# Keys and queries turned for a recurrence: one half of the partitions copied by ScalarE, the other by a transfer, and the order of steps laid out anew

## What is computed

```python
def step(S, inp):                      # S: [b, 16 heads, 2, 16]
    ct, st, kt, vt, bt = inp           # kt: the key of this token, 16 values a head
    S0, S1 = (S[:, :, 0], S[:, :, 1])
    Sd = jnp.stack([ct * S0 + st * S1, -st * S0 + ct * S1], axis=2)
    pred = jnp.einsum('bhsd,bhd->bhs', Sd, kt)
    Sn = Sd + bt * (vt - pred)[..., None] * kt[:, :, None, :]
    return (Sn, Sn)
_, Ys = jax.lax.scan(step, S0, xs)     # over all tokens, in order
retrieved = jnp.einsum('blhsd,blhd->blhs', Y, Q) * sel_C_gate[..., None]
```

## Time and profile before

| | us |
|---|---|
| median of 3 runs | 3696.65 (3696.49 to 3699.05) |
| the profiled execution | 3695.73 |
| its span, first to last instruction | 3693.9 |
| stage of layers 0 to 2 side by side | about 95 to 2143 |
| one unit in its steady part | 235.5 |

### The profile page before, as it was taken

The page is one execution under the profiler, slowest core; times in us unless marked ns, Lnnn a source line. Parts: engine busy times, 40 slices in busy tenths (PEclk is TensorE's granted clock), DMA queues, the critical chain, the costliest instruction groups (busy, mean ns, idle before and its releaser), DMA issues.

```text
span 3693.9 us, 39884 instructions
## 1 busy us (share of the span) xinstructions
PE 2537.0 (69%) x13729; PEld 1367.2 (37%) x13729; DVE 2599.1 (70%) x5721; ACT 1670.5 (45%) x3056; POOL 509.9 (14%) x530
## 2 busy tenths in 40 slices
PE   3587967768677687686633047773577787778788
PEld 1343333333333333333211012221355555555553
DVE  3478758989889889797877656664366666666663
ACT  1233343442534424345243224444366666666662
POOL 0000003030030200301111200003112121212120
PEclk9589778878678687796866567787699999999999
DMA  2000000100001000010000021102677777777651
GB/s 82 2 9 27 22 27 6 45 2 26 23 3 49 1 22 28 1 43 7 30 7 15 1 79 29 29 6 98 180 205 208 203 214 201 218 211 201 198 160 53
DMA packets 310336, 274.34 MB, mean 74 GB/s; under 512 B 16012, under 2 KB 285982, under 8 KB 309718
## 3 DMA queue, kind: packets, MB, share of 16 engines
q1 hardware_dynamic: 310134, 271.79, 25.4%
HBM read 149.39 MB, written 122.36 MB: 74 GB/s over the span
## 4 chain that ended last, share of the span: by engine, by line
DVE 36%; PE 30%; issue 14%; ACT 13%; POOL 5%; DMA 1%; SPq 1%; DVEq 0%; POOLq 0%; ACTq 0%
ACT t L1364 3%; DVE t L2496 3%; PE banks L2519 3%; PE banks L2563 3%; ACT t L2431 2%; PE banks L420 2%; DVE t L1147 1%; PE banks L2480 1%; POOL t L2463 1%; DVE t L787 1%; DVE t L1660 1%; DVE t L1664 1%; DVE t L2249 1%; ACT L145 1%; DVE t L786 1%
## 5 line engine op out<-in xcount | busy, mean ns | idle before, releaser
L2496 DVE CUSTOM_DVE_ANT_0 t<-banks,t 128x896 f32<-128x896 f32 (+7 forms) x512 | 381.8, 753 | 147.2 <-PE banks L2482 76.4
L2519 PE MATMUL banks<-ident,t 128*128 128x128 f32 x2304 | 392.4, 291 | 134.8 <-ACT xT L2534 46.2
L2507 ACT ACTIVATE t<-t 128x896 f32<-128x896 f32 (+7 forms) x512 | 398.6, 779 | 175.6 <-DVE t L2496 175.0
L2519 PEld LDWEIGHTS banks<-ident,t 128*128 128x128 f32 x2304 | 260.4, 145 | 242.1 <-ACT xT L2534 62.3
L2463 POOL TENSOR_TENSOR t<-t 128x512 f32<-128x512 f32 x96 | 122.3, 1274 | 797.0 <-DMA t<-relative_scratch 724.6
L1700 ACT ACTIVATE t<-t 128x16 f32<-128x16 f32 x256 | 82.6, 323 | 316.0 <-DVE t L1664 254.2
L2480 PE MATMUL banks<-t 128*128 128x512 bf16 (+3 forms) x768 | 216.1, 337 | 7.2 <-DVE t L2496 7.0
L145 ACT ACT_TABLE_LOAD x112 | 143.7, 1283 | 152.4 <-DVE t L578 32.2
L538 POOL TENSOR_TENSOR t<-t 128x512 f32<-128x512 f32 x28 | 50.2, 1793 | 993.3 <-ACT t L510 993.3
L1095 ACT ACTIVATE t<-banks 128x512 f32<-128x512 f32 x128 | 76.2, 595 | 219.6 <-PE banks L1061 219.3
L1066 PE MATMUL banks<-t 128*128 128x512 f32 x256 | 146.9, 657 | 37.4 <-DVE t L1143 31.4
(11 more groups left out here) (451 smaller groups left out, 6196.5 us busy)
## 6 DMA issues: line engine op xcount, KB each, us to landing
relative_scratch<-t SPq DMA_DIRECT2D x128, 512.0 KB, 5.1
t<-relative_scratch SPq DMA_DIRECT2D x128, 512.0 KB, 4.4
relative_scratch<-t SPq DMA_DIRECT2D x128, 256.0 KB, 5.4
t<-in_wmoe SPq DMA_DIRECT2D x64, 384.0 KB, 3.0
t<-relative_scratch SPq DMA_DIRECT2D x80, 256.0 KB, 2.9
t<-cut_scratch SPq DMA_DIRECT2D x192, 64.0 KB
cut_scratch<-t SPq DMA_DIRECT2D x8, 768.0 KB, 3.4
z_scratch<-t SPq DMA_DIRECT2D x8, 512.0 KB, 3.0
```

Source lines behind the costliest of these rows:

```text
L2496: nc.vector.tensor_tensor_reduce(s.s[z][:, 0:n], ps[:, b0:b0 + 1 + i // 4, :].rearrange("p b n -> p (b n)")[:, 0:n], s.bias[r][:, j, WIDE ...
L2507: nc.scalar.activation(s.s[z][:, 0:n], s.s[z][:, 0:n], ACT.Exp, scale=-1.0, bias=s.least[:, z:z + 1]).then_inc(*a.mark("weights", u))
L2519: nc.tensor.transpose(ps[:, 4 + c % 2, (t - lo) * P:(t - lo + 1) * P], s.s[u % NS][:, t * P:(t + 1) * P], k.ident[:]).then_inc(*e.mark("tu ...
```

## The change

ACT's copies are halved: each bank is copied once, to partitions 0 to 63, and with its loops turned round: for each token four neighbouring features, so that it writes 16 bytes at a stretch and reads PSUM at steps of 512 bytes. Partitions 64 to 127 of kc and qc are filled by one transfer each, issued by SP in a new part turn2_sp: keys after the last of the keys' copies, queries after the last of the queries'. DVE's first reads of keys and of queries wait for these transfers in place of the copies. The strings of PE, ACT, DVE and SP are new throughout; SP's has two more steps t in each unit, behind the stores of in2 and ahead of back's. The string of POOL is unchanged. Of the strings only SP's and the steady lines of ACT's stand here.

```diff
--- before.py
+++ after.py
@@ -1360,9 +1360,17 @@
             act.wait_ge(e, u, w, n)
             if u:
                 act.wait_ge(k.line("rec_dve"), "ret", u - 1)
-            for half in (slice(0, H2), slice(H2, P)):
-                nc.scalar.copy(out[half, :, d0:d0 + 4].rearrange("p t d -> p d t"),
-                               ps[0:H2, G0 + n].rearrange("p (d t) -> p d t", d=4)).then_inc(*a.mark(u, w, n))
+            nc.scalar.copy(out[0:H2, :, d0:d0 + 4], ps[0:H2, G0 + n].rearrange("p (d t) -> p t d", d=4)).then_inc(
+                *a.mark(u, w, n))
+
+
+def turn2_sp(k, s):
+
+    for u in range(UNITS0):
+        for w, x in enumerate((s.kc, s.qc)):
+            yield
+            k.sp.wait_ge(k.line("turn2_act"), u, w, 3)
+            k.nc.sync.dma_start(x[H2:], x[0:H2]).then_inc(*k.queue(f"both{w}").mark(u))
 
 
 
@@ -1586,7 +1594,7 @@
 
 
 def rec_dve(k, s, u):
-    nc, dve, v, a, n = k.nc, k.dve, k.line("rec_dve"), k.line("turn2_act"), u % 2
+    nc, dve, v, n = k.nc, k.dve, k.line("rec_dve"), u % 2
     stt, tt, copy, reduce = (nc.vector.scalar_tensor_tensor, nc.vector.tensor_tensor, nc.vector.tensor_copy,
                              nc.vector.tensor_reduce)
     if u == 0:
@@ -1610,7 +1618,7 @@
         tt(later[:, :, c], later[:, :, c + 1], dl[:, :, c], ALU.mult).then_inc(*v.mark())
     yield
     dve.wait_ge(v)
-    dve.wait_ge(a, u, 0, 3)
+    dve.wait_ge(k.queue("both0"), u)
     tt(rows[:, :, :, 0:DH2], kb, rep(s.coef[:, :, 0], 3, DH2), ALU.mult).then_inc(*v.mark())
     yield
     tt(s.kd[:], kb, rep(later[:, :, 1:], 3, DH2), ALU.mult).then_inc(*v.mark())
@@ -1676,7 +1684,7 @@
         tt(y[:, :, j], y[:, :, j], s.at, ALU.add).then_inc(*v.mark())
         prior = y[:, :, j]
     yield
-    dve.wait_ge(a, u, 1, 3)
+    dve.wait_ge(k.queue("both1"), u)
     tt(y[:, :, BS - 1], s.first[:, 1:, 0:DH2], qb[:, :, BS - 1], ALU.mult).then_inc(*v.mark())
     yield
     dve.wait_ge(v)
@@ -1768,57 +1776,57 @@
 TURNS_ACT = (
-    "emrraeraremaeraeerererermerereerererearerremreeriirrrriairiramiiriirriarriiiiriiiimmrimimgmgmgmttttttttmbmmggfgb"
-    "ggkmkfmmfafmfmmfmfeememerarearemareaeerererermerererereereraerreremreiirrrrriairiramiiriirriarriiiiriiiimmrimimg"
...
+    "bkfkafmfmmfmmfmmffeememearearemareaererererermerererereereraererremreirirrririariamriiirirriaririiiriiiimmrgmmig"
+    "igmmmttttmttttbgmgmgbggfkkmmmfafmmfmfmfmmfeeeemaeararermaeerreerremreerererererereareerremreirirrriririarariimri"
+    "mirrimmrariiriiiiiigmimiggttttttttmggbmgggmmbkfkafmfmmfmmfmmffeememearearemareaererererermerererereereraererremr"
...
 )
...
@@ -1829,7 +1837,8 @@
 )
 
 TURNS_SP = (
-    "ibwqqwwwqqwwwwwwwqwwwwwwwwwiiiqwwwwwwwwiiibqwwwwwwwwiiibqqwwwwwwwwiiibwwwwwwwwiiibwwwwwwwwiiibwwwwwiiibiiibb"
+    "btiwqqwwwqqwwwwwwwwqwwwwwwwwiiiqttwwwwwwwwiiittbqwwwwwwwwiiittbqqwwwwwwwwiiittbwwwwwwwwiiittbwwwwwwwwiiittbwwwww"
+    "iiibttiiitbtb"
 )
 
 
@@ -1923,7 +1932,7 @@
 
 
 def side_by_side_sp(k, s, keep):
-    in_turn(TURNS_SP, {"in2": inputs2_sp(k, s, keep), "experts": experts1_sp(k, s), "turn0": turn0_sp(k, s),
+    in_turn(TURNS_SP, {"in2": inputs2_sp(k, s, keep), "experts": experts1_sp(k, s), "turn0": turn0_sp(k, s), "turn2": turn2_sp(k, s),
                        "back": back_sp(k, s, keep)})
```

More of the change, by code:

```diff
@@ L1776 @@
[L1776 to L1780, removed]
@@ L1781 @@
-    "eaaaaeaeaeeaaieeeeaeeeeeeeeeeeeeeeeeeeeeeeeeeeeeeeeeeeeeeeeeeeeeeeeiiiiiiittttbtttbtggaaaaiiiiiiiittttbtttbtggbb"
+    "bfatgmiemmmfmmmmmmffffmmfffmmmmfmmmmmmfmmfmmmmmmmmmmmmmmmmemfmmffffmfffmfmmfmfmmeemmammmmmmemmaammmmmmmmaemaeeem"
+    "eeeeeeeeeeemmemmmemmemeememeeeeeeeemmmmmemmemeeeeemeeeemmeeeemmeemeemeeeaeeemeeaeefamaimfmfffmfffmfmfmmfmmmmemmm"
+    "emmmaeaammmmmmmmammaeeeeeeeeemmmmmmmeeeeeeemeeeeeeemmeeeeeeeeemmemmmeeeemmmeeeeeeeeeeeeemeeeeeeemimimmimmemiiiim"
+    "ttttttttmfgmgmfaaaamfffimfffmmfmfmfmmmmmmeemmaeaaaeaeemmmmmmmeemeeeeeeeeeeemmeeeeeeeeemmemeeeemeeeeeeemmmeeeeeee"
@@ new lines @@
+    "meeeeeeemmeeeeeemimmmmimmmmiiiiimmttttttttmmbmembgfmgaaaaffffimfffmmfmmfmfeeaemmaaeaeeeaemmeeeemmmmmmeeeeeeemmee"
+    "eeeeeeeeeeeemmmmeeeeeeemmmeeeeeeemeeeeeeemmeeeeeemmmimmmimmmmimmmmmmmmiiiimmmttttmmbmettttmbfmggaaamfafffmmfiffm"
+    "fmmffmmeeaeammmmmmmmaaemmeeeammmemmmmmeeeemeeemeeeeeeeeeeemmmmmmeeeeeeemmeeeeeeemeeeeeeeeeeeeeemeeeeeemmmimmmimm"
+    "miiiiimmttttttttmmbmembgfmgaaaaffffimfffmmfmmfmfeeaemmaaeaeeeaemmeeeemmmmmmeeeeeeemmeeeeeeeeeeeeeemmmmeeeeeeemmm"
+    "eeeeeeemeeeeeeemmeeeeeemmmimmmimmmmimmmmmmmmiiiimmmttttmmbmettttmbfmggaaaamfffifmfffmmfmmffmmeeaeammmmmmmmaaemme"
@@ L1795 @@
+    "rereraereiiriaririarriiiirarriiiriiiriiirgrrrrrrrrrrrrrrrrgigibgggtbggttkttkttatiiiiiiiiiiiiiiiiiiggigirrgrgrgrg"
+    "grrrrrrrrrrrrrrrrrrrrrrrrrrrttbttttbttkkrrrrrrrrrrrrrrrrrrrrrrrrrrrrrrrrbb"
 )
 TURNS_DVE = (
[L1798 to L1800 removed]
@@ L1821 @@
-    "rrgrgrrrrrrrrrrrrrrrrrrrrrrrrrrrrrrrrrrrrrrrrrrrrrrrrrrrrrrrrrrrrrrrrrrrrrrrrrrrrrrrrrrrrrrrrrrrrrrrrrrrrrrrrrrr"
+    "bffagmmiermmmfffffffmffmmmmmffmfmffffffmfffmffmfffmfmffmffmmmmmfmmmmmmmmmmmmmffffffmfmffmffffffffffffffffffffffm"
+    "mmmmemmmeaammeemeemememeaeeaemammaeaeaemaemaeamaeaeaaeamamemamaemaeameeaaaemameaeaameaaeameaamemammaaeaaemaeaaea"
+    "fmafmfafffafaafmfffffffffffffffffffffmfmffmmmmmmemmmemmeeemeaeaememeaememamaemeaeaeaeaaaeaeamemaaeaemamaemaeaaem"
+    "aeaeaeamaemaeaeeaaeeamaeaaeaiaaamiiamamaimmiaiimiiimmiiigiiiigigmgggggggggfggggggggggfffffffffrrrrrrraaafmffmfff"
@@ new lines @@
+    "fmfmfmfffmffmfffffmfffrrrrrrrermrmrmrermrerererererermererererarmraerarerarerermrmrerarerarermrarermrmreraraermr"
+    "arerarerarerarerararerarerarerararerararerarermrmrerarermrarermrmrarerarmrairarrrrrrrrrrrrrrrrrmrmrrrrrrrirrrirr"
+    "rrrrrararararariririririririrmrarrrrrrrararirarirararirgririrarirririrmgagagggggfggggmmbmmbgbgggggggggmffffffmfr"
+    "frfrmraraarfrffmfffffffffffffffffffrrrrmrmrrerrrmermrrerererererermerererermrmrarermrarerarerarerarermrmrerarerm"
+    "rarermrmreraraermrerararerarerarerararerarerarerararerararerarermrmrerarermrarermrmrarerarmrairarrrrrrrrrrrrrrrr"
@@ new lines @@
+    "rmrmrmrrirrmrmrirarmrarararariririririririrmrmrarrrrararirarirarariraririrmrgrariririrmrgrgrrgrgrmgmgmmgaggggfbg"
+    "bgbggmggggggffffffmfmfrfrrrmrarrfafaffffffffffffffffffffmmrrrmrmremrrmrmrermrerererererererererermrmrarmrmermrar"
+    "mrarerarermrermrmrarerarermrmrerarermraraererarerararerarerarmrermrarerarerarermrarerarerararerarerarerarermrmra"
+    "rerarmrairarrrrrrrrrrrrrrrrrmrmrrrrirrrirrrrrrrararararariririririririrmrarrrrrrrararirarirararirgririrarirririr"
+    "mgagagggggfggggmmbmmbgbgggggggggmffffffmfrfrfrmraraarfrffmfffffffffffffffffffrrrrmrmrrerrrmermrrerererererermere"
@@ new lines @@
+    "rerermrmrarermrarerarerarerarermrmrerarermrarermrmreraraermrerararerarerarerararerarerarerararerararerarermrmrer"
+    "arermrarermrmrarerarmrairarrrrrrrrrrrrrrrrrmrmrmrrirrmrmrirarmrarararariririririririrmrmrarrrrararirarirararirar"
+    "irirmrgrariririrmrgrgrrgrgrmgmgmmgaggggfbgbgbggmggggggffffffmfmfrfraraarmrrfrfffffffffffffffffffffmmrrrmrmremrrm"
+    "rmrermrerererererererererermrmrarmrmermrarmrarerarermrermrmrarerarermrmrerarermraraererarerararerarerarmrermrare"
+    "rarerarermrarerarerararerarerarerarermrmrarerarmrairarrrrrrrrrrrrrrrrrmrmrrrrirrrirrrrrrrararararaririririririri"
@@ new lines @@
+    "rmrarrrrrrrararirarirararirgririrarirririrgmgaggaggggebgbgbgmgmgmggggggggeeererererererreaeeaaaaeaeaeaeaearerera"
+    "raererarererarerererarererarerarerarerarerararerarerararerarerairarararararrrrrrrrrirrrirararararararrririririri"
+    "ririrarararirararirarirargririrarrrrrrrrrrrrrrrrrrrrrrrrrrrrrrrrrrrrrrrrrrrrrrrrrrrrrrrrrrrrrrrrrrrgrgrgrgrgrgrr"
+    "grgrgigigbibgbgggggggggrrrrairarriiiiiiiiirrrrirrririrrgrririrrgrgrgrgrgrgrgrgrgrgrgririrgrgrgrgrgrgrgrgrirgrgrr"
+    "rrrrrrrrrrrrrrrrrrrrrrrrrrrrrrrrrrrrrrrrrrrrrrrrrrrrrrrrrrrrrrrrrrrrrrrrrrrrrrrrrrrrrrrrrrrrrrrrrrrrrrrrrrrrrrrr"
```

40 lines of the change are left out of this document (7 added, 33 removed).

## The result

| | before | after |
|---|---|---|
| median, us | 3696.57 (3688.74 to 3699.05) | 3567.88 (3551.71 to 3570.01) |
| span of the profiled execution | 3693.9 | 3567.9 |
| TensorE's granted clock over the span | 0.815 | 0.828 |

The ratio is 0.9646, 95% interval 0.9614 to 0.9678: 129 us faster. The forecast was 3614 us and the range 3586 to 3642.

A forecast was written before the change was run, and what follows sets the result against it. No engine was full; DVE was nearest to the bound, waiting 9.7 us a unit behind ACT's block of copies. 80 us for the shorter block plus 3 for the order gave 3614 us, range 3586 to 3642.

The forecast's parts named there:

- Part 1: ACT's copies at the turn: 8 of 16 a unit go, block 16.6 to 8.3 us, 66 us in all.
- Part 2: Remaining copies, reshaped: about 0.6 us each, block about 5.8 us; with Part 1, 80 us off.
- Rival 1: Copies at the turn: scattered PSUM read costs what the scattered write did, copies stay 1.0 us; 3630 us, chance 0.28.
- rival 4: Copies at the turn: scattered read costs several ns an element, so slower; 3724 us at 2.5 us a copy, chance 0.05.
- Part 3: SP's two 512 KB transfers a unit: 5.7 us each with issue, covered by other work, cost 0.
- Part 4: New order of steps around the turn: about 0.5 us a unit, some 3 us gained in the steady units.
- an allowance of 3 us a unit: Rest of the new order, effect on other idle time not derivable: 3 us a unit either way, 24 us.
- two differences around the turn: L205's place at the turn: norm up to 2.4 us earlier in one unit kind, 1.3 us later in the other.
- the order gains more: New order gains beyond the block, 3 us a unit from other idle time; 3590 us, chance 0.12.
- under the same dependencies: Argument against the order gaining beyond the block: the old order was laid out under the same dependencies.
- the 21 us of other waits a unit: DVE's other idle time a unit, largest wait 4.1 us; the new order's effect on it could not be derived.

The follow-up runs named there:

- e1: Kernel before with the new copies and transfers, but the old order of PE, ACT and DVE; 3615.3 us, ratio 0.9765.
- e4: Kernel before with only the loop order of its sixteen copies a unit changed to token by token; 3645.4 us, ratio 0.9858.
- e2: Kernel after in its new order, but with the sixteen old copies a unit and no transfers; 3644.4 us, ratio 0.9861.
- e8: e1 with DVE's sums of squares (L1315) spread over the other steps in units 1 to 5; 3619.2 us, ratio 0.9774.
- e11: New copies and transfers, the new order only up to 139 us, the old order from there; 3602.7 us, ratio 0.9750.
- a2: Kernel after, unchanged, run once more; 3564.6 us, ratio 0.9637.

## Why the prediction was wrong

**Part 1, half the copies, and the block: right.** Forecast 5.8 us, measured 5.9. The queries' copies are paced by PE's transposes as worked out (L1363 waits 0.26 and 0.28 us for L1351). e1 is the kernel that this part describes, and it took 3615 us. Its profiled execution is 76 us shorter than that of before, and the "ret" times say how they were made: 9.4 us a steady unit for 9.7 forecast, 9.3 in unit 5, 11.5 and 12.0 in the last two for 10.8, 6.0 in the first for 9.7.

**Part 2, the shape: right.** About 0.6 us forecast, 0.581 measured. The scattered PSUM read costs nothing that can be seen: 578 ns in e4 against 577 for a contiguous copy. Rival 1 and rival 4 fall. The Trainium skill (SBUF — State Buffer, Door 1: The DMA port swizzle) states that SBUF has lines of 16 bytes and that an access which crosses to a new line pays. The writes agree: 16 bytes at a stretch show no cost, and floats 64 bytes apart cost 436 ns. The same passage gives PSUM lines of 8 bytes, and what it names as slowed by a pattern that isn't contiguous there are matmuls. The prediction carried this over to ScalarE's reads, and these runs show no price for them.

**Part 3, the transfers: right.** 4.2 us from issue to landing for 5.7 forecast with the issue, and no wait for them.

**Part 4, the order: wrong, and all of the error.** 3 us forecast, with an allowance of 3 us a unit, 24 us; measured 47 to 52 us (e1 to after, e2 to before). The step that failed is the one that put the order at 3 us and its reach at 24: it went by two differences around the turn and by the dependencies, left the waits away from the turn at nothing but an allowance either way, and had no term for the start. The runs put 24 us in four steady units and 33 ahead of the first "ret" in its place. It failed in three ways.

First, it priced only what stands around the turn in a steady unit. The 660 us from 95 us to the first "ret", where DVE was idle 162 us in e1 and 130 us after, had no term. 33 us of the gain lie there. 24.5 of them stand before unit 0's keys are turned for the first time (L1363 starts at 537.6 us in e1 and at 513.1 in after), and 8.2 come from a handful of steps ahead of 139 us. The rival "the order gains more" counted 3 us a unit over eight units and so had no place for it either.

Second, "under the same dependencies" was taken as a reason that the 21 us of other waits a unit would stay. e8 shows it true of one edit by hand; with the whole new order the unit is 6.0 us shorter than with the new copies alone (226.1 in e1, 220.1 in after). That an order is tight against single moves is no evidence that it is the best one.

Third, the granted clock was taken as given, as the trace of before had it (0.78 a unit). Identical steps took 221.9 or 229.0 us a unit at clocks of 0.84 and 0.76, and e1 and e8, with the same lists, are 8 us apart from 620 to 712 us. A range needs room for this, and it can fall either way.

The chances were 0.12 for a gain of the order beyond the block, and no rival went beyond 24 us, though 0.15 to 0.2 was put outside the range. With every string laid out anew and 31 us idle in each unit of the nearest engine, the allowance should have reached to the idle time that the trace shows, 21 us a unit and the start's, with a good part of the chance.

## What to carry over

Price an edit by its own wait and its cover; that worked here (80 us forecast, 81 between the medians, 76 between the profiled executions). When a change also lays out all in-order queues anew, take that as a term of its own: read the start-up stage too, and look where an engine waits for one part while the step of another part could come first, if its producer on the other engine is moved as well (PE at L691 for DVE's L302, with L448 and DVE's L604 behind). In e11 the 8.2 us won at such a place near the start were all there 360 us later.

Before a difference of a few us between two profiles is given a cause, look for the first instruction where their lists part. A lead that grows ahead of it, as in e8, has another cause, and the granted clock of that stretch is the first thing to read.

## Not expected of the hardware

ScalarE copies 64x512 floats from PSUM with reads 512 bytes apart in 578 ns, as fast as contiguous (577 ns), but writes them 64 bytes apart in SBUF in 1013 ns. A transfer of 512 KB from 64 partitions to the other 64 lands 4.2 us after its issue. The granted clock can differ between executions of the same instructions: 31 matmuls took 12.5 us in e1 at 0.56 and 7.7 us in e8 at 0.95, with the same lists on every engine up to there. Yet the profiled executions of after and a2, the same kernel, agree in every unit to 0.1 us (220.9, 219.3, 221.0, 219.3), clock included, and differ by 6.7 us in the later stages.
